# A residual block of two quantised 3x3 convolutions on one core: second weights transposed between the phases, the last phase's loads reordered, one totals addition moved

## The chip, the cores and the metric

The kernel runs on one core of one Trainium2 chip. The metric is the device time of one execution in microseconds (us).

## What is computed

The input x has 32 images of 128 channels and 56 by 56 pixels, all float32. Two convolutions of 3x3 taps (padding 1) follow one another; their weights are rounded to eight integer levels (-4 to 3) times a step alpha. Behind each stands a batch normalisation over all images, so that no image of the second convolution can start before the last of the first is done.

```
residual = x
out = conv3x3_decomposed(x, lsq_quantize(w1, alpha1))
out = jax.nn.relu(batchnorm(out, gamma1, beta1))
out = conv3x3_decomposed(out, lsq_quantize(w2, alpha2))
out = batchnorm(out, gamma2, beta2)
out = jax.nn.relu(out + residual)
```

## The kernel before, in words

The channels lie on the 128 partitions. An image is one row of 3136 float32 per partition. Ten slots in SBUF hold images; the other 22 results of each convolution are spilled to DRAM and come back.

**Phases.** Phase 1 is the first convolution for images 0 to 31, phase 2 the second (steps 32 to 63). The last phase applies the second normalisation, adds x, applies ReLU and stores. Between phases 1 and 2, `batchnorm_affine` (L767) makes scale and bias from the totals.

**One image.** Rows 0 to 35 are computed by a Winograd scheme with six products, rows 36 to 55 directly in three chunks of nine taps. Every operand is split into a high and a low part (`v_hi`, `v_lo`, `d_hi`, `d_lo`), so each tap is two matmuls. TensorE runs `chunk` (L914, 54 matmuls) into PSUM banks 6 and 7 and `products` (L886, 36 matmuls) into banks 0 to 5. VectorE (`step`, L750) makes `q_rows`, `p_rows` and `v_rows` of the next image, the low parts `d_lo` (L691) and of the first pair `v_lo` (L686), and from the products the output rows: `first_difference` (L697), `second_difference` (L705), `second_sum` (L711), `rows_out` (L716). `add_totals` (L737) adds an image's sums to the totals; it needs ScalarE's three squares of that image (L512). ScalarE (`step`, L521) copies chunks and products out of PSUM, squares, and casts the high parts. GpSimd subtracts the low parts of the second and third pair (L422), two instructions per image.

**Weights.** VectorE rounds the weights to integers in bfloat16 and sums taps for the Winograd scheme (`sum_taps`, L257; for w2 in images 3 to 8). TensorE transposes them in lots (`transpose_lot`, L879) into PSUM, and ScalarE copies them to `w1T` or `w2T` with a scale (`take`, L438). w2 has three lots of 8, 8 and 5 transposes, all into bank 7. In before they stand in images 10, 11 and 12 of phase 1, behind the last chunk (`lot_of_w2`, L946), and the next image's first chunk, which needs bank 7, waits for the copies (L964). ScalarE takes them behind the high parts of the next image (L538).

**Order of the work.** Each engine's program is written by hand, with semaphores counted up. Explicit images come first (`EXPLICIT` = 14 for all three engines), then a loop of two images a turn. SyncE issues the transfers strictly in its own order: an instruction that waits holds up all behind it. In the last phase the x of 32 images is loaded into seven buffers, `xbuf`. They lie over memory of the convolutions, and each load waits for its last use (L368 to L391):

```
AT = [0, PIX, 2 * PIX, 3 * PIX, 4 * PIX, 5 * PIX]
TEMPS = 5 * PIX + 2 * ((D_PLANE + 7) // 8 * 8)
xbuf = [placed(f"xbuf{b}", PIX, F32, b * PIX)[:, :] for b in range(ARENA_XBUFS)]
xbuf.append(nc.alloc_sbuf_tensor_at("xbuf_w2", [C, PIX], F32, offset=w2_base)[:, :])
```

`AT` holds the places of `w1T`, `q_rows` and `p_rows`, `v_rows`, `v_hi`, `v_lo`, and the two `d` planes; `m1`, `m3`, `d1`, `s1` begin at `TEMPS`. So buffer 5 lies over `d_hi`, `d_lo`, `m1` and part of `m3`, and buffer 6 over `w2T`. `FINAL` (L268) is the order of the last phase; image j of it uses buffer j % 7. `load_y2` (L363) reloads a spilled result into the slot of image j - 6 as soon as that one's output is stored.

Of the kernel before, what the change touches and what calls it, by code (L numbers as in the profile page):

```python
# [27 lines left out]
def residual_block(nc, x, w1, alpha1, gamma1, beta1, w2, alpha2, gamma2, beta2, out):  # L28
# [48 lines left out]
    with ExitStack() as ctx:  # L77
# [32 lines left out]
        xbuf.append(nc.alloc_sbuf_tensor_at("xbuf_w2", [C, PIX], F32, offset=w2_base)[:, :])  # L110
# [125 lines left out]
        W_BANK = [[0, 1, 2, 3], [7, 7, 7]]  # L236
        W2_FIRST = 10
        EXPLICIT = 14
# [45 lines left out]
        def _(sp):  # L284
# [91 lines left out]
            load_residual(2)  # L376

            sp.wait_ge(chunk_done, STEPS * NC)
            sp.wait_ge(sums_ready, STEPS * SR)
            load_residual(5)  # L380

# [3 lines left out]
            for b in range(2):  # L385
                sp.wait_ge(y2_stored[b], 16 * (SPILL // 2))


            sp.wait_ge(m_done, STEPS * M)
            sp.wait_ge(chunk_done, STEPS * NC)  # L390
# [43 lines left out]
        def _(act):  # L434
# [86 lines left out]
            def step(g, p, b, phase, first=False, second=False, last=False, input_ready=None, relu_next=None,  # L521
                     w2_lot=None):
                if not last:
                    input_ready()
                    hi_direct(g + 1, p + 1)
                take_chunk(g, p, b, NC - 1)
                take_m(g, 0)
                if second:
                    act.wait_ge(shift_ready, phase + 1)
                if not first:  # L530
                    square(g - 1, p + (SLOTS - 1), 1 - b, phase, 0)
                take_m(g, 1)
                if not first:
                    square(g - 1, p + (SLOTS - 1), 1 - b, phase, 1)
                    square(g - 1, p + (SLOTS - 1), 1 - b, phase, 2)
                if not last:
                    hi_pairs(g + 1)
                if w2_lot is not None:  # L538
                    take_w2(w2_lot)
                if relu_next is not None:  # L540
                    relu_next()
                if not last:

                    if not first:
                        act.wait_ge(totalled, g)
                    for j in range(NC - 1):
                        take_chunk(g + 1, p + 1, 1 - b, j)
# [18 lines left out]
            for n in range(2, EXPLICIT):  # L566
                phase1(n, n % 2, n // 2, w2_lot=n - W2_FIRST if n in range(W2_FIRST, W2_FIRST + 3) else None)
            with act.Fori(EXPLICIT // 2, (IMAGES - 2) // 2) as i:
                for b in range(2):
                    phase1(i * 2 + b, b, i)  # L570
            phase1(IMAGES - 2, 0, (IMAGES - 2) // 2)
            step(IMAGES - 1, IMAGES - 1, 1, 0, last=True)
            finish_phase(IMAGES - 1, IMAGES - 1, 1, 0)

# [52 lines left out]
        def _(dve):  # L627
# [122 lines left out]
            def step(g, p, b, phase, first=False, input_ready=None):  # L750
# [7 lines left out]
                if not first:  # L758
# [4 lines left out]
                rows_out(g, p, b)  # L763
                if first:
# [113 lines left out]
        def _(pe):  # L878
# [67 lines left out]
            def lot_of_w2(n):  # L946
                def transposes(j):
                    if j == NC - 1:
                        pe.wait_ge(w_int_ready[1], 2)
                        pe.wait_ge(evac_done, n * NC + 2)  # L950
                        transpose_lot(1, n - W2_FIRST)
                return transposes
# [8 lines left out]
            for n in range(1, EXPLICIT):  # L961
                if n in range(W2_FIRST + 1, W2_FIRST + 4):

                    pe.wait_ge(wT_ready, TAKES + (2, 5, TAKES)[n - 1 - W2_FIRST])  # L964
                convolve(n, wT[0], lot_of_w2(n) if n in range(W2_FIRST, W2_FIRST + 3) else None)
            with pe.Fori(EXPLICIT // 2, IMAGES // 2) as i:
                for b in range(2):
                    convolve(i * 2 + b, wT[0])
            convolve(IMAGES, wT[1])
# [25 lines left out]
```

## Time and profile before

| what | value |
|---|---|
| median of 3 runs | 1489.55 us (1488.96 to 1489.67) |
| the profiled execution's own time | 1491.95 us |
| its span, first to last instruction | 1490.0 us |
| TensorE busy | 1136.8 us, 76% |
| VectorE busy | 1141.8 us, 77% |
| ScalarE busy | 855.4 us, 57% |
| GpSimd busy | 306.3 us, 21% |
| HBM read and written | 174.59 MB and 122.03 MB |

The profile is one execution. Its busy time is the time in which an engine had an instruction in work, and its times count from the first instruction. "Idle before" an instruction is put down to what it waited for last. The engines are named PE (TensorE), PEld (its weight loads), DVE (VectorE), ACT (ScalarE), POOL (GpSimd) and SP (SyncE); a q behind the name is the engine's queue that issues transfers.

### The profile page before, as it was taken

How to read it: one execution, taken by the hardware profiler on the slowest of the kernel's cores; microseconds unless marked ns; L12 is line 12 of the kernel's file. 1: busy time of each engine (PE TensorE's matmuls, PEld its weight loads, DVE VectorE, ACT ScalarE, POOL GpSimd, SP SyncE). 2: the span in 40 equal slices, each digit the busy share in tenths (PEclk: the TensorE clock that was granted, in tenths of full speed). 3: DMA queues.
4: the chain of work that ended last, by engine and by line, in shares of the span. 5: the costliest groups of instructions: out<-in, count | busy, mean ns of one | idle time of the engine just before them, and what ended most of it. 6: DMA issues, size and time to landing. Idle time of an engine off the chain costs nothing.

```text
span 1490.0 us, 18697 instructions
## 1 busy us (share of the span) xinstructions
PE 1136.8 (76%) x5802; PEld 1033.1 (69%) x5802; DVE 1141.8 (77%) x1626; ACT 855.4 (57%) x1263; POOL 306.3 (21%) x147
## 2 busy tenths in 40 slices
PE   5999998999999999699999999999999400000000
PEld 5999987999999998699999999999999400000000
DVE  7999996788888886898888888888888632322324
ACT  3555555555556565677777777777777532222224
POOL 3333221122222222322222222222222100000000
PEclk9999999999999999899999999999999855555555
DMA  3455443455542220022244455554230699999999
GB/s 162 168 189 196 184 173 118 152 196 187 198 186 86 86 86 0 1 87 87 86 172 172 172 194 194 192 196 170 89 129 5 246 428 430 430 430 430 429 429 408
DMA packets 28110, 297.00 MB, mean 199 GB/s; under 512 B 3888, under 2 KB 3888, under 8 KB 4912
## 3 DMA queue, kind: packets, MB, share of 16 engines
q1 hardware_dynamic: 22608, 245.25, 41.7%
q10 hardware_dynamic: 5472, 51.38, 8.1%
q8 instruction: 15, 0.25, 0.1%
q14 instruction: 15, 0.12, 0.0%
HBM read 174.59 MB, written 122.03 MB: 199 GB/s over the span
## 4 chain that ended last, share of the span: by engine, by line
issue 64%; DMA 18%; POOL 14%; DVE 1%; ACT 1%; POOLq 1%; ACTq 0%; DVEq 0%
POOL v_lo L422 14%; DMA slots<-conv_spill 10%; DMA out<-slots 4%; DMA xbuf<-in_x 3%; DVE slots L872 1%; ACT slots L619 1%; POOLq L427 0%; POOLq L421 0%; POOLq L77 0%; POOLq L422 0%; ACTq L623 0%; DVE affine L793 0%; DVE tiny L790 0%; DVE affine L792 0%; POOL ident L408 0%
## 5 line engine op out<-in xcount | busy, mean ns | idle before, releaser
L422 POOL TENSOR_TENSOR v_lo<-v_rows,v_hi 128x1008 fp32r<-128x1008 f32 x128 | 304.0, 2395 | 835.1 <-ACT v_hi L474 835.1
L925 PE MATMUL conv_psum<-d_hi,w1T 128*128 128x398 f32 (+2 forms) x864 | 289.0, 338 | 11.0 <-ACT w2T L440 8.1
L925 PE MATMUL conv_psum<-d_hi,w2T 128*128 128x398 f32 (+2 forms) x864 | 285.8, 335 | 12.4 <-DVE d_lo L691 12.4
L925 PE MATMUL conv_psum<-d_lo,w1T 128*128 128x398 f32 (+2 forms) x864 | 286.6, 336 | 0.0
L925 PE MATMUL conv_psum<-d_lo,w2T 128*128 128x398 f32 (+2 forms) x864 | 284.1, 333 | 0.0
L512 ACT ACTIVATE squares<-slots,minus_shift 128x1008 bf16 (+3 forms) x192 | 225.0, 1172 | 13.7 <-ACT squares L512 8.9
L905 PE MATMUL conv_psum<-v_lo,w1T 128*128 128x512 f32 x576 | 227.1, 394 | 0.0
L905 PE MATMUL conv_psum<-v_lo,w2T 128*128 128x512 f32 x576 | 227.0, 394 | 0.0
L905 PE MATMUL conv_psum<-v_hi,w2T 128*128 128x512 f32 x576 | 226.8, 394 | 0.3 <-POOL v_lo L422 0.2
L905 PE MATMUL conv_psum<-v_hi,w1T 128*128 128x512 f32 x576 | 226.8, 394 | 0.0
L619 ACT ACTIVATE slots<-slots,affine 128x3136 f32<-128x3136 f32 (+1 forms) x34 | 93.6, 2754 | 209.1 <-DVE slots L872 208.3
L872 DVE SCALAR_TENSOR_TENSOR slots<-slots,affine,xbuf 128x3136 f32<-128x3136 f32 (+1 forms) x30 | 97.4, 3265 | 151.4 <-DMA slots<-conv_spill 146.7
L493 ACT ACTIVATE slots<-conv_psum 128x392 f32 (+3 forms) x192 | 91.4, 476 | 187.8 <-PE conv_psum L925 186.6
L474 ACT CAST v_hi<-v_rows 128x1008 fp32r<-128x1008 f32 x192 | 186.1, 1028 | 6.7 <-DVE v_rows L673 5.8
L691 DVE TENSOR_TENSOR d_lo<-slots,d_hi 128x1176 fp32r<-128x1176 f32 x64 | 90.7, 1416 | 110.3 <-ACT d_hi L479 110.3
L925 PEld LDWEIGHTS conv_psum<-d_hi,w1T 128*128 128x128 f32 x864 | 165.2, 191 | 14.0 <-ACT w2T L440 9.4
L925 PEld LDWEIGHTS conv_psum<-d_hi,w2T 128*128 128x128 f32 x864 | 163.2, 189 | 14.1 <-DVE d_lo L691 12.8
L925 PEld LDWEIGHTS conv_psum<-d_lo,w1T 128*128 128x128 f32 x864 | 165.6, 192 | 1.2
L925 PEld LDWEIGHTS conv_psum<-d_lo,w2T 128*128 128x128 f32 x864 | 163.6, 189 | 1.2
L479 ACT CAST d_hi<-slots 128x1176 fp32r (+1 forms) x64 | 75.6, 1180 | 139.0 <-PE conv_psum L925 133.5
L649 DVE SCALAR_TENSOR_TENSOR q_rows<-slots 128x2016 f32 (+1 forms) x64 | 144.3, 2255 | 0.8 <-ACT slots L518 0.5
L905 PEld LDWEIGHTS conv_psum<-v_lo,w1T 128*128 128x128 f32 x576 | 108.7, 189 | 24.1
(79 smaller groups left out, 1511.3 us busy)
## 6 DMA issues: line engine op xcount, KB each, us to landing
conv_spill<-slots SPq DMA_DIRECT2D x44, 1568.0 KB, 6.1
slots<-conv_spill SPq DMA_DIRECT2D x44, 1568.0 KB, 10.8
slots<-in_x SPq DMA_DIRECT2D x31, 1568.0 KB, 8.9
out<-slots ACTq DMA_DIRECT2D x30, 1568.0 KB, 11.7
xbuf<-in_x SPq DMA_DIRECT2D x28, 1568.0 KB, 52.0
xbuf_w<-in_x SPq DMA_DIRECT2D x4, 1568.0 KB, 51.6
out<-slots ACTq DMA_DIRECT2D x4, 784.0 KB, 10.5
slots<-in_L_conv_w SPq DMA_DIRECT2D x2, 576.0 KB, 9.7
```

Source lines behind the costliest of these rows:

```text
L422: nc.gpsimd.tensor_tensor(pair_window(1, k), pair_rows(k), pair_window(0, k).bitcast(F32), ALU.subtract).then_inc(pool_lo_ready, 1)
L474: nc.scalar.copy(pair_window(0, k), pair_rows(k)).then_inc(hi_ready, 1)
L479: nc.scalar.copy(window(d_plane[0], 0, D_ROWS), rows_of(slot(p + SLOTS, WINO - 1))).then_inc(hi_ready, 1)
L493: nc.scalar.activation(rows_of(slot(p + SLOTS, r0, r1)), bank_rows(CHUNK_BANK[j], r1 - r0), ACT.Identity, accum_out=sums[b][:, col:col + 1 ...
L512: nc.scalar.activation(into, y, ACT.Square, bias=minus_shift[:, phase:phase + 1], accum_out=sums[b][:, col:col + 1]).then_inc(squared, 1)
L619: nc.scalar.activation(z, z, ACT.Relu, bias=affine[:, 1, 1:2]).then_inc(final_ready, 1)
L649: return nc.vector.scalar_tensor_tensor(out=out, in0=in0, scalar=scalar, in1=in1, op0=ALU.mult, op1=ALU.add)
L691: nc.vector.tensor_tensor(window(d_plane[1], 0, D_ROWS), rows_of(slot(p, WINO - 1)), window(d_plane[0], 0, D_ROWS).bitcast(F32), ALU.subtr ...
L872: nc.vector.scalar_tensor_tensor(out=z, in0=z, scalar=affine[:, 1, 0:1], in1=xbuf[b][:, r0 * W:r1 * W], op0=ALU.mult, op1=ALU.add).then_in ...
L905: last = nc.tensor.matmul(bank_run(M_BANK[k], TILES), w[:, M_WEIGHT[k] + kw, :], run(v_plane[half], k * TILES, (k + 1) * TILES, kw - 1), s ...
L925: last = nc.tensor.matmul(bank_run(CHUNK_BANK[j], r1 - r0), w[:, kh * 3 + kw, :], run(d_plane[half], r0 - WINO + 1, r1 - WINO + 1, kw - 1) ...
```

## The change

The three lots of w2 leave phase 1. TensorE transposes them behind the last image of phase 1, into banks 6, 7 and 0, and ScalarE copies them behind its last squares. Images 2 to 31 of TensorE and ScalarE are now turns of the loop, on VectorE images 10 to 31. The buffer over `w2T` becomes number 5, and the one over `d_hi`, `d_lo`, `m1` and `m3` number 6; the last loads are issued in the order 3, 4, 5, 6. In the last step of each phase the totals of the image before are added behind the output rows.

```diff
-        xbuf.append(nc.alloc_sbuf_tensor_at("xbuf_w2", [C, PIX], F32, offset=w2_base)[:, :])
+        xbuf.insert(5, nc.alloc_sbuf_tensor_at("xbuf_w2", [C, PIX], F32, offset=w2_base)[:, :])
...
-        W_BANK = [[0, 1, 2, 3], [7, 7, 7]]
-        W2_FIRST = 10
-        EXPLICIT = 14
+        W_BANK = [[0, 1, 2, 3], [6, 7, 0]]
+        EXPLICIT = 10
...
             load_residual(2)
+            for b in range(2):
+                sp.wait_ge(y2_stored[b], 16 * (SPILL // 2))
 
             sp.wait_ge(chunk_done, STEPS * NC)
-            sp.wait_ge(sums_ready, STEPS * SR)
-            load_residual(5)
-
             sp.wait_ge(m_done, STEPS * M)
             load_residual(3)
             load_residual(4)
-            for b in range(2):
-                sp.wait_ge(y2_stored[b], 16 * (SPILL // 2))
-
-
-            sp.wait_ge(m_done, STEPS * M)
-            sp.wait_ge(chunk_done, STEPS * NC)
+            load_residual(5)
+
+            sp.wait_ge(sums_ready, STEPS * SR)
             load_residual(6)
...
-                if w2_lot is not None:
-                    take_w2(w2_lot)
...
-            for n in range(2, EXPLICIT):
-                phase1(n, n % 2, n // 2, w2_lot=n - W2_FIRST if n in range(W2_FIRST, W2_FIRST + 3) else None)
-            with act.Fori(EXPLICIT // 2, (IMAGES - 2) // 2) as i:
+            with act.Fori(1, (IMAGES - 2) // 2) as i:
...
             finish_phase(IMAGES - 1, IMAGES - 1, 1, 0)
+            for h in range(3):
+                take_w2(h)
...
-                if not first:
+                if not first and input_ready is not None:
                     add_totals(g - 1, 1 - b, phase)
                 if input_ready is not None:
                     lo_of_pair(g + 1, 0)
                 second_sum(g)
                 rows_out(g, p, b)
+                if input_ready is None:
+                    add_totals(g - 1, 1 - b, phase)
...
+            def second_weights():
+
+                pe.wait_ge(w_int_ready[1], 2)
+                pe.wait_ge(evac_done, IMAGES * NC)
+                pe.wait_ge(m_copied, IMAGES * 2 - 1)
+                for h in range(3):
+                    transpose_lot(1, h)
+                pe.wait_ge(wT_ready, 2 * TAKES)
...
             convolve(0, wT[0], rest_of_w1)
-            for n in range(1, EXPLICIT):
-                if n in range(W2_FIRST + 1, W2_FIRST + 4):
-
-                    pe.wait_ge(wT_ready, TAKES + (2, 5, TAKES)[n - 1 - W2_FIRST])
-                convolve(n, wT[0], lot_of_w2(n) if n in range(W2_FIRST, W2_FIRST + 3) else None)
-            with pe.Fori(EXPLICIT // 2, IMAGES // 2) as i:
+            convolve(1, wT[0])
+            with pe.Fori(1, IMAGES // 2) as i:
                 for b in range(2):
                     convolve(i * 2 + b, wT[0])
+            second_weights()
             convolve(IMAGES, wT[1])
```

TensorE, in image 10 of phase 1 in the program before (`ident,w_int` is a transpose of w2's integers):

```order
L925 MATMUL conv_psum<-d_hi,w1T 128x284
L925 MATMUL conv_psum<-d_lo,w1T 128x284
L882 MATMUL conv_psum<-ident,w_int 128x128 [waits evac_done,w2_int_ready]
L882 MATMUL conv_psum<-ident,w_int 128x128 x7
L905 MATMUL conv_psum<-v_hi,w1T 128x512 [waits m_copied,lo_ready]
L905 MATMUL conv_psum<-v_lo,w1T 128x512
```

The eight transposes stand between the last chunk and the products; images 11 and 12 have the same piece. In the changed program these images have no such rows.

TensorE, the end of phase 1's loop and the start of phase 2 in the changed program:

```order
L899 MATMUL conv_psum<-v_lo,w1T 128x512
L957 REGISTER_ALU
L957 COMPARE_AND_BRANCH
L876 MATMUL conv_psum<-ident,w_int 128x128 [waits m_copied,evac_done,w2_int_ready]
L876 MATMUL conv_psum<-ident,w_int 128x128 x20
L919 MATMUL conv_psum<-d_hi,w2T 128x398 [waits evac_done,lo_ready,wT_ready]
L919 MATMUL conv_psum<-d_lo,w2T 128x398
```

The lots stood between chunks and products of three images; now all 21 transposes stand behind the loop, and only the first chunk of phase 2 waits for wT_ready.

ScalarE, the end of phase 1 and the start of phase 2 in the changed program (`squares,sums` are the last squares, `slots<-slots,affine` is the ReLU of phase 2):

```order
L507 ACTIVATE squares,sums<-slots,minus_shift 128x1120 [waits evac_done,squared]
L507 ACTIVATE squares,sums<-slots,minus_shift 128x1008 [waits rows_ready,squared] x2
L435 ACTIVATE w2T<-conv_psum 128x1024 [waits transposed]
L435 ACTIVATE w2T<-conv_psum 128x384
L435 ACTIVATE w2T<-conv_psum 128x128 [waits transposed]
L435 ACTIVATE w2T<-conv_psum 128x768
L435 ACTIVATE w2T<-conv_psum 128x128
L435 ACTIVATE w2T<-conv_psum 128x640 [waits transposed]
L513 ACTIVATE slots<-slots,affine 128x1176 [waits affine_ready]
L474 CAST d_hi<-slots 128x21x56 [waits chunk_done,relu_ready]
L513 ACTIVATE slots<-slots,affine 128x1960
```

In the program before, the ReLU with its wait for affine_ready stood right behind the last squares; the six copies are new here.

SyncE, the loads of the first seven images' x for the last phase (`xbuf_62` is buffer 0, `xbuf_w_68` the one over w2T, `xbuf_67` the one over d_hi, d_lo, m1 and m3), in the program before:

```order
L361 DMA xbuf_62<-in_x 128x3136 [waits m_done]
L361 DMA xbuf_63<-in_x 128x3136 [waits v_ready]
L361 DMA xbuf_64<-in_x 128x3136 [waits pool_lo_ready,lo_ready]
L361 DMA xbuf_67<-in_x 128x3136 [waits sums_ready,chunk_done]
L361 DMA xbuf_65<-in_x 128x3136 [waits m_done]
L361 DMA xbuf_66<-in_x 128x3136
L361 DMA xbuf_w_68<-in_x 128x3136 [waits m_done,chunk_done,y2_stored1,y2_stored0]
L361 DMA xbuf_62<-in_x 128x3136 [waits added]
```

The load of buffer 5 with its wait for sums_ready stands ahead of those of buffers 3 and 4.

And in the changed program:

```order
L360 DMA xbuf_62<-in_x 128x3136 [waits m_done]
L360 DMA xbuf_63<-in_x 128x3136 [waits v_ready]
L360 DMA xbuf_64<-in_x 128x3136 [waits pool_lo_ready,lo_ready]
L360 DMA xbuf_65<-in_x 128x3136 [waits chunk_done,m_done,y2_stored1,y2_stored0]
L360 DMA xbuf_66<-in_x 128x3136
L360 DMA xbuf_w_68<-in_x 128x3136
L360 DMA xbuf_67<-in_x 128x3136 [waits sums_ready]
L360 DMA xbuf_62<-in_x 128x3136 [waits added]
```

The wait for sums_ready stood ahead of four loads and now stands ahead of one.

## Rows read from the trace of the kernel before

**Rows 1.** The page, the span in 40 slices: busy share of the DMA engines.

```profile
DMA  3455443455542220022244455554230699999999
```

**Rows 2.** Busy time by stage: PE, PEld, DVE, ACT, POOL, clock, DMA share, GB/s.

```profile
215.00:220.00 5.00, 4.19 (x15) 4.18 (x16) 4.90 (x11) 0.76 (x2) 3.40 (x2) 0.66 0.96 326
335.00:580.00 245.00, 245.00 (x1257) 223.08 (x1256) 216.10 (x335) 143.03 (x252) 60.83 (x29) 1.00 0.34 127
1170.00:1175.00 5.00, 2.97 (x13) 2.08 (x11) 3.80 (x9) 4.20 (x8) 0.00 (x0) 1.00 0.00 2
1180.00:1490.00 310.00, 0.00 (x0) 0.00 (x0) 112.19 (x38) 93.63 (x34) 0.10 (x1) 0.50 1.00 426
```

**Rows 3.** Who waited for whom, TensorE only: total, times, longest us.

```profile
PE conv_psum L925 <- ACT w2T L440: 8.1, 3, 3.0
```

**Rows 4.** Timeline of TensorE, images 9 to 31: start us, length us.

```profile
186.19 0.39 PE L905 MATMUL conv_psum<-v_hi,w1T 128*128 128x512 f32 x1
...
194.53 0.35 PE L925 MATMUL conv_psum<-d_hi,w1T 128*128 128x398 f32 x1
...
203.76 0.62 PE L882 MATMUL conv_psum<-ident,w_int 128*128 128x128 bf16 x8
...
215.81 0.70 PE L925 MATMUL conv_psum<-d_hi,w1T 128*128 128x398 f32 x1 [3.02 <-ACT w2T L440]
...
288.68 0.39 PE L905 MATMUL conv_psum<-v_hi,w1T 128*128 128x512 f32 x1
...
587.31 0.39 PE L905 MATMUL conv_psum<-v_hi,w1T 128*128 128x512 f32 x1
```

**Rows 5.** Timeline of TensorE, the start of phase 2.

```profile
608.24 0.70 PE L925 MATMUL conv_psum<-d_hi,w2T 128*128 128x398 f32 x1 [12.42 <-DVE d_lo L691]
```

**Rows 6.** Timeline of ScalarE, the copies of the three lots of w2.

```profile
214.37 1.39 ACT L440 ACTIVATE w2T<-conv_psum 128x1024 fp32r<-128x1024 bf16 x2
...
237.22 1.13 ACT L440 ACTIVATE w2T<-conv_psum 128x128 fp32r<-128x128 bf16 x3
...
259.70 0.69 ACT L440 ACTIVATE w2T<-conv_psum 128x640 fp32r<-128x640 bf16 x1
```

**Rows 7.** Timeline of VectorE and ScalarE, from phase 1 to phase 2.

```profile
593.15 0.69 DVE L709 TENSOR_TENSOR conv_psum<-m,conv_psum 128x504 f32<-128x504 f32 x1 [1.48 <-PE conv_psum L905]
594.73 0.17 DVE L740 TENSOR_TENSOR totals<-totals,sums 128x10 f32<-128x10 f32 x1 [0.90 <-ACT squares L512]
594.82 0.68 DVE L714 TENSOR_TENSOR conv_psum<-m,conv_psum 128x504 f32<-128x504 f32 x1
...
604.20 1.37 ACT L518 ACTIVATE slots<-slots,affine 128x1176 f32<-128x1176 f32 x1 [3.60 <-DVE affine L793]
```

**Rows 8.** Timeline of TensorE and VectorE, the end of phase 2.

```profile
1172.58 0.39 PE L905 MATMUL conv_psum<-v_lo,w2T 128*128 128x512 f32 x1
...
1174.36 0.67 DVE L649 SCALAR_TENSOR_TENSOR s<-conv_psum,s 128x504 f32<-128x504 f32 x1
```

**Rows 9.** Timeline of SyncE's queue, the first loads of the last phase.

```profile
1175.11 0.80 SPq L361 DMA_DIRECT2D xbuf<-in_x  x2
...
1184.87 0.33 SPq L361 DMA_DIRECT2D xbuf<-in_x  x1
```

**Rows 10.** Timeline of GpSimd and VectorE, images 9 to 16.

```profile
189.34 1.38 DVE L691 TENSOR_TENSOR d_lo<-slots,d_hi 128x1176 fp32r<-128x1176 f32 x1
195.52 5.36 POOL L422 TENSOR_TENSOR v_lo<-v_rows,v_hi 128x1008 fp32r<-128x1008 f32 x2 [12.21 <-ACT v_hi L474]
195.90 1.84 DVE L740 TENSOR_TENSOR totals<-totals,sums 128x10 f32<-128x10 f32 x1
...
213.00 0.16 DVE L740 TENSOR_TENSOR totals<-totals,sums 128x10 f32<-128x10 f32 x1
213.61 4.79 POOL L422 TENSOR_TENSOR v_lo<-v_rows,v_hi 128x1008 fp32r<-128x1008 f32 x2 [12.73 <-ACT v_hi L474]
...
315.68 4.41 POOL L422 TENSOR_TENSOR v_lo<-v_rows,v_hi 128x1008 fp32r<-128x1008 f32 x2 [13.15 <-ACT v_hi L474]
```

More of the change, by code:

```diff
@@ L519, in relu, with step @@
                                      scale=affine[:, 0, 0:1]).then_inc(relu_ready, 1)
-            def step(g, p, b, phase, first=False, second=False, last=False, input_ready=None, relu_next=None,
-                     w2_lot=None):
+            def step(g, p, b, phase, first=False, second=False, last=False, input_ready=None, relu_next=None):
                 if not last:
@@ L944, in rest_of_w1 @@
                     pe.wait_ge(wT_ready, TAKES)
[L946 to L952, printed above, removed]
+            def second_weights():
[5 more added lines that the diff above has]
+                pe.wait_ge(wT_ready, 2 * TAKES)
             pe.wait_ge(ident_ready, 1)
```

## The prediction

> **What bounds the kernel now.** I read the bands of the page first, then the busy time by stage, then who waits for whom, and last the timelines at the three places that the change touches. The DMA band [rows 1] shows a kernel of two kinds: 31 slices with the DMA engines partly idle, then a last phase in which they are full. The table by stage [rows 2] says the same: between 335 and 580 us TensorE is busy for 245.00 of 245 us, and from 1180 us on it is not used and the DMA share is 1.00. So the convolutions last as long as TensorE's instructions plus its waits, and the last phase as long as its bytes plus its late start. Whatever gives TensorE a wait back, or starts the last phase's transfers sooner, should show in the end; most other edits should not.
>
> TensorE's waits on the way are few: 8.1 us in three pieces for the copies of w2T [rows 3], and 12.42 us between the phases for the first d_lo [rows 5].
>
> **Term 1, the lots of w2 leave images 10 to 12.** The first matmul of products marks each image [rows 4]. From image 14 to image 31 it moves 587.31 - 288.68 = 298.63 us over 17 images, 17.567 us each. From image 9 to image 14 it moves 102.49 us where five such images take 87.83. The excess, 14.66 us, is what the three lots cost, more than the 8.1 us of waits. The rest has two parts. One is the transposes themselves: the eight of a lot take 0.62 us at 203.76, so all 21 take under 1.9 us. The other is the clock: the first wait ends at 215.81, and from 215 to 220 us the mean granted clock is 0.66 [rows 2], that is, a part of them at 1.2 GHz instead of 2.4. These matmuls follow one another at twice their distance until the clock is back. All of it goes with the lots, since nothing else in images 10 to 12 has been added and TensorE, as the bound, passes it on in full. **-14.66 us.**
>
> The unrolled images become turns of a loop on TensorE and ScalarE (from image 2) and on VectorE (from image 10). In before, images 14 to 31 are such turns, and TensorE is busy for every one of 245 us of them, so the loop itself costs nothing that can be seen; I cost it at nothing, with a small rival below.
>
> **Where the lots go.** The 21 transposes stand behind the last products, under 1.9 us of an idle stretch of 12.42 us [rows 5]. The six copies take 1.39 + 1.13 + 0.69 = 3.21 us [rows 6]. They stand on ScalarE between the last square of phase 1 and the first ReLU, where it waited 3.60 us for the affine numbers [rows 7]. Term 2 brings the last square and the affine numbers forward by the same amount, so the cover stays 3.60 us and 0.39 us of it is left. The transposes are done before the last squares are, so the copies need not wait. Cost 0; without the cover it is the 3.21 us of the copies, in front of the ReLU, the first d_hi, the first d_lo and so TensorE. A gain here is excluded: ScalarE waits there either way. TensorE's new wait for all copies ends some 4 us before that d_lo.
>
> **Term 2, the totals of the last image but one.** In the last step VectorE reaches this addition with its first difference done at 593.15 + 0.69 = 593.84 us and waits for a square until 594.73; the second sum follows at 594.82 [rows 7]. Without the addition in front, the second sum needs only the difference before it. The nearest dependent pair is in [rows 8]: an operation ends at 1174.36 + 0.67 = 1175.03, and SyncE, which waits for its semaphore, issues at 1175.11 [rows 9], 0.08 us later; I take 0.1. The second sum then starts at 593.95, 0.87 us sooner, and the four output rows, the last square, the last totals, the affine numbers and the first ReLU of phase 2 with it. The moved addition (0.17 us) comes behind the last rows, while ScalarE squares; hidden. **-0.87 us** at the first boundary. The same happens at the second boundary, but behind it the DMA engines set the end, not the affine numbers, so I count nothing there.
>
> **Term 3, loads of the last phase.** In before, load 5 stood ahead of 3 and 4 and waited for the very last use of s1; SyncE takes its instructions in order, so all four loads are issued from 1175.11 on [rows 9]. From 1170 to 1175 us the DMA share is 0.00 [rows 2]. Now 3, 4 and 5 need only the last matmul, which ends at 1172.58 + 0.39 = 1172.97 us [rows 8]; with 0.1 us for the semaphore they are issued from 1173.07, and only load 6 waits for s1. Three loads are 4.8 MB, at the 426 GB/s of [rows 2] some 11 us of work, so load 6 and the load issued at 1184.87 [rows 9] find the engines still busy, as before. Each image's output is then issued faster than it is stored. The queue never runs dry, the bytes are the same, and the end moves by the start: 1175.11 - 1173.07 = **-2.04 us**. At worst this is 0, if something other than bytes sets the pace of the last phase. At best the 0.87 us of term 2 are worth something too. The waits for stores of y2, moved ahead, are for transfers issued long before: nothing.
>
> **Sum.** -14.66 - 0.87 - 2.04 = -17.57 us. The profiled execution took 1491.95 us with a span of 1490.0 us, so it would take 1474.4 us. The median of the runs shown, 1489.55 us, is 2.4 us below the profiled one; I take the same difference off it: **1472.0 us**.
>
> **Rivals.**
> 1. The copies lie open. The slack is 0.39 us, worked out from three copies' groups in another place. For it: ScalarE also has to see the semaphores of three lots. Against it: all of these are up when it arrives. Time 1472.0 + 3.2 = 1475.2 us. Chance 7%.
> 2. The reordered loads bring nothing, because the last phase is tied by its chain of add, ReLU, output and reload of a slot. For it: VectorE waits for reloads there all the time. Against it: the DMA share is 1.00 all along. Time 1474.0 us. Chance 7%. With rival 1 together 1477.2 us.
> 3. The change doesn't do what it says for phase 1: the three lots gave VectorE time to catch up, and without them TensorE waits elsewhere. For it: in images 3 to 9 VectorE runs late. Its totals addition takes 1.84 us at 195.90, while GpSimd's subtraction has run since 195.52, against 0.16 us at 213.00 [rows 10]. Against it: that image was reached before the first stall, which ends at 215.81, so VectorE had caught up by itself; from 195.90 to 213.00 it took 17.10 us, 0.47 us less than TensorE's 17.57. But without the transposes GpSimd would start at 195.52 + 17.57 = 213.09 instead of 213.61, only 0.09 us behind that addition. Being late costs nothing at first: d_lo was done at 190.72 us, and TensorE takes it up at 194.53, a cushion of 3.8 us. If VectorE stays late in a milder way, 1 or 2 us are lost: 1473.5 us, chance 4%.
> 4. **The slow end.** The same lateness feeds itself: two VectorE subtractions of each image come to stand behind a whole GpSimd subtraction of 4.41 / 2 = 2.2 us. Its round is then 17.10 - 1.68 + 4.4 = 19.8 us, 2.25 us over TensorE's, in 22 images (10 to 31) 49.6 us, less the cushion 45.8 us: 1472.0 + 45.8 = 1518 us. It turns the gain into a loss from (17.57 + 3.8) / 22 = 0.97 us an image on. Against it: images 3 to 9 were late with one such block and a round below 17.57 us, and later GpSimd's pair takes 4.41 us, unhindered. Chance 2%.
>
> The Trainium skill ("SBUF — State Buffer", section "Who interferes with whom") states the rule behind rivals 3 and 4: a VectorE instruction with two SBUF inputs and a GpSimd instruction that reads SBUF share a port under an exclusive lock, and the later one waits for the whole of the earlier. By that rule the 0.09 us decide who waits, and the time would go towards rival 4 if VectorE lost each time. The row with 1.84 us agrees with the lock; the full rounds of TensorE through images 3 to 9 speak against a cost.
>
> **How the numbers follow.** My forecast has 78%, rivals 1 to 4 have 7, 7, 4 and 2%, and 2% is left for things not thought of. The forecast's own spread is about 1 us each way, for the offset to the median, the length of the slow clock behind the first wait of phase 2, and the tail; term 2 counted twice gives 1471.1. With rivals 1 and 2, together too, the range is **1469.5 to 1477.2 us**. About 0.2% (3 us) is what a measurement of this kernel can tell from no change. All cases but the fourth and part of the unknown are faster by more: faster 0.96, same 0.01, slower 0.03.
>
> **What would show it.** Right: images 9 to 14 at 17.57 us each, no wait of TensorE for w2T, the granted clock whole in phase 1; the six copies between 599.7 and 603.3 us of the old times, which is 14.66 us earlier in the new profile, followed by a small wait of ScalarE for the affine numbers; the second sum right behind the difference; three residual loads some 0.1 us after the last matmul, and no idle slice of DMA behind them. Wrong: totals additions of 1.8 us and longer past image 9, a ReLU that starts when the last copy ends, or a DMA share under 1.00 in the last phase.

## The result, and the profile after

| what | before | after |
|---|---|---|
| median | 1489.61 us (1488.96 to 1489.82) | 1474.51 us (1474.09 to 1474.73) |
| the profiled execution's own time | 1491.95 us | 1474.38 us |
| its span | 1490.0 us | 1472.6 us |

The ratio is 0.9899 (95% interval 0.9882 to 0.9916): 15.1 us faster. The forecast was 1472.0 us, with 1469.5 to 1477.2 as its range. The profiled executions are 17.57 us apart, which is the forecast's sum to the hundredth; the medians are not. Both facts are looked into below: the agreement to the hundredth is partly luck, and the difference between profile and median belongs to the first term.

The page after, of the two bands that answer to [rows 1]:

```profile
PEclk9999999999999999899999999999999755555555
DMA  4354454444452210022245555444230799999999
```

The last phase still begins in the 32nd slice, and its first slice is fuller (7 for 6). By stage, to be held against [rows 2] (columns as there):

```profile
200.00:560.00 360.00, 360.00 (x1848) 327.97 (x1847) 327.56 (x498) 208.74 (x368) 92.33 (x41) 1.00 0.39 147
1163.00:1168.00 5.00, 0.00 (x0) 0.00 (x0) 4.29 (x10) 0.00 (x0) 0.55 (x1) 0.52 1.01 432
1180.00:1470.00 290.00, 0.00 (x0) 0.00 (x0) 96.69 (x30) 84.07 (x31) 0.00 (x0) 0.50 1.01 429
```

TensorE is busy for 360.00 of 360 us, with a granted clock of 1.00, where [rows 2] had 0.66 from 215 to 220 us. Its waits after, as [rows 3]:

```profile
PE conv_psum L876 <- DVE slots L250: 12.5, 1, 12.5
PE conv_psum L919 <- issue: 10.3, 1, 10.3
PE conv_psum L919 <- ACT slots L488: 1.4, 1, 1.4
PE conv_psum L919 <- ACT w1T L435: 1.2, 1, 1.2
PE conv_psum L899 <- POOL v_lo L417: 0.2, 1, 0.2
```

The waits for w2T, 8.1 us, are gone, and no wait in images 1 to 31 has come in their place. The first, third and fourth rows are the start of the kernel, the last is image 33. The second is the boundary between the phases: 21 transposes and 10.34 us idle where [rows 5] had 12.42. The timeline of TensorE there:

```profile
581.65 1.35 PE L876 MATMUL conv_psum<-ident,w_int 128*128 128x128 bf16 x21
593.33 0.67 PE L919 MATMUL conv_psum<-d_hi,w2T 128*128 128x398 f32 x1 [10.34 <-issue]
```

ScalarE, which answers to [rows 6] and the last of [rows 7]:

```profile
585.55 3.01 ACT L435 ACTIVATE w2T<-conv_psum 128x1024 fp32r<-128x1024 bf16 x6
589.24 1.37 ACT L513 ACTIVATE slots<-slots,affine 128x1176 f32<-128x1176 f32 x1 [0.68 <-DVE affine L787]
```

The six copies take 3.01 us where 3.21 was forecast, and ScalarE still waits 0.68 us for the affine numbers. VectorE, the first difference and second sum of [rows 7], and the moved addition:

```profile
579.13 0.69 DVE L701 TENSOR_TENSOR conv_psum<-m,conv_psum 128x504 f32<-128x504 f32 x1 [1.48 <-PE conv_psum L899]
579.85 0.69 DVE L706 TENSOR_TENSOR conv_psum<-m,conv_psum 128x504 f32<-128x504 f32 x1
...
584.24 0.17 DVE L732 TENSOR_TENSOR totals<-totals,sums 128x10 f32<-128x10 f32 x1
```

The sum starts 0.03 us behind the end of the difference (0.1 was forecast). SyncE's queue at the start of the last phase, as [rows 9]; the last matmul of phase 2 ends at 1158.02:

```profile
1158.12 0.80 SPq L360 DMA_DIRECT2D xbuf<-in_x  x2
1158.97 0.43 SPq L360 DMA_DIRECT2D xbuf_w<-in_x  x1
1159.44 9.85 SPq L360 DMA_DIRECT2D xbuf<-in_x  x2
```

Three loads go out from 0.10 us behind that end, as forecast. GpSimd in images 13 to 15 and VectorE's totals additions in images 11 and 13, for [rows 10]:

```profile
266.54 5.37 POOL L417 TENSOR_TENSOR v_lo<-v_rows,v_hi 128x1008 fp32r<-128x1008 f32 x2 [11.89 <-ACT v_hi L469]
284.12 5.28 POOL L417 TENSOR_TENSOR v_lo<-v_rows,v_hi 128x1008 fp32r<-128x1008 f32 x2 [12.21 <-ACT v_hi L469]
301.67 4.41 POOL L417 TENSOR_TENSOR v_lo<-v_rows,v_hi 128x1008 fp32r<-128x1008 f32 x2 [12.28 <-ACT v_hi L469]
```

```profile
231.75 1.89 DVE L732 TENSOR_TENSOR totals<-totals,sums 128x10 f32<-128x10 f32 x1
...
266.80 1.97 DVE L732 TENSOR_TENSOR totals<-totals,sums 128x10 f32<-128x10 f32 x1
```

In this execution VectorE stayed late without the lots, as rivals 3 and 4 feared: pairs of 5.3 us go on to image 14, and totals additions of over 1.8 us stand in images 11 and 13. The prediction had named such additions past image 9 as a sign that it was wrong. TensorE's full 360 us say that they cost nothing. They are no mark of the change either: the changed kernel profiled once more, in the same span within 0.1 us, is not late at all.

```profile
266.62 4.42 POOL L417 TENSOR_TENSOR v_lo<-v_rows,v_hi 128x1008 fp32r<-128x1008 f32 x2 [13.14 <-ACT v_hi L469]
```

### The profile page after: what moved, and what is told of

Same layout as the page of the kernel before. It is cut to its first block, busy times and chain, and to the rows that moved or that the text cites. A ratio compares the mean times of both kernels' runs of the same rounds, so it can differ in the third digit from the quotient of the medians.

```text
span 1472.6 us, 19012 instructions
## 1 busy us (share of the span) xinstructions
PE 1132.3 (77%) x5802; PEld 1030.2 (70%) x5802; DVE 1150.9 (78%) x1626; ACT 855.3 (58%) x1263; POOL 306.7 (21%) x147
## 4 chain that ended last, share of the span: by engine, by line
issue 62%; DMA 18%; POOL 14%; DVE 2%; ACT 2%; PE 1%; POOLq 1%; SPq 0%; ACTq 0%; DVEq 0%
POOL v_lo L417 14%; DMA slots<-conv_spill 11%; DMA out<-slots 4%; DMA xbuf<-in_x 3%; DVE slots L866 1%; ACT slots L611 1%; PE conv_psum L919 1%; DMA slots<-in_L_conv_w 0%; POOLq L422 0%; ACT v_hi L469 0%; ACT w1T L435 0%; DVE slots L250 0%; POOLq L416 0%; PE conv_psum L876 0%; ACT d_hi L474 0%
## 5 line engine op out<-in xcount | busy, mean ns | idle before, releaser
L919 PE MATMUL conv_psum<-d_hi,w2T 128*128 128x398 f32 (+2 forms) x864 | 285.9, 335 | 10.3 <-issue 10.3
```

What stands on the lines that cost most here:

```text
L919: last = nc.tensor.matmul(bank_run(CHUNK_BANK[j], r1 - r0), w[:, kh * 3 + kw, :], run(d_plane[half], r0 - WINO + 1, r1 - WINO + 1, kw - 1) ...
```

## The experiments

All times are medians. Ratios are to runs of the kernel before made beside them on the same chip; those had medians of 1490.22 us beside the first four kernels below, 1490.08 beside the next four, 1489.88 beside the three with or next to the warm boundary and 1489.96 beside the last. Single executions of the kernel before scatter from 1489.0 to 1494.5 us. "Marks" are the starts of an image's first products matmul in the timeline, as in the prediction. A "slow" matmul is one of TensorE's chunks (128x398 and smaller) that takes over 0.5 us where most take 0.35; the granted clock is then at the lower of its two levels, 1.2 GHz.

### The same program again

Unchanged code.

> The kernel before once more, unchanged, for a second profiled execution beside the first. The measured change was -15.1 us in the runs' medians, while the two profiled spans lie 1490.0 - 1472.6 = 17.4 us apart, close to the -17.57 us that was forecast. Theory A (the profiled execution of before was an unlucky one: its TensorE spent longer at 1.2 GHz behind the stalls of the three w2 lots than usual): a new profiled span near 1487.7 us, and images 9 to 14 take some 12.3 us more than five steady ones, not 14.66. Theory B (the three lots always cost 14.66 us, and the changed kernel lost some 2.4 us elsewhere): a span near 1490 us again in profiled executions, or images 9 to 14 at 14.7 us of excess again at a shorter span.

**Measured:** 1489.78 us (1489.09 to 1493.94), ratio 0.9999 (0.999 to 1.0008), span 1487.8 us, 2.2 us under the first profile of the same program. The excess of images 9 to 13 over 87.83 us is 11.86 us, not 14.66. That is 2.80 us less where the span is 2.2 us less; image 0 took 0.52 us more this time (its products begin at 28.61 us and not at 28.09). The windows around the second lot's stall show why. First the kernel before in its first profile, then in this one (columns: PE, clock, DMA share, GB/s):

```profile
236.00:244.00 8.00, 5.60 (x22) 0.79 1.00 376
```

```profile
236.00:244.00 8.00, 5.24 (x29) 1.00 0.98 370
```

The wait is 2.76 us in both timelines. Behind it the granted clock fell in one execution and not in the other.

### One part of the change alone

Lots and loops only:

```diff
-        xbuf.insert(5, nc.alloc_sbuf_tensor_at("xbuf_w2", ...
+        xbuf.append(nc.alloc_sbuf_tensor_at("xbuf_w2", ...
...
-                if not first and input_ready is not None:
+                if not first:
                     add_totals(g - 1, 1 - b, phase)
...
-                if input_ready is None:
-                    add_totals(g - 1, 1 - b, phase)
```

(against the changed kernel, with the loads too in their old order).

> Only the three lots of w2 moved behind phase 1 (with the loops as in the change); loads and totals as before. Theory A: -12.3 us or so against before in the medians (ratio 0.9917). Theory B: -14.7 us (0.9901). Rival of the exposed copies: the last totals come 0.87 us later than in the change, but so do the affine numbers, so the copies stay under the wait of 3.6 us; if they lay open, 3 us less gain.

Totals only, against before:

```diff
-                if not first:
+                if not first and input_ready is not None:
                     add_totals(g - 1, 1 - b, phase)
...
                 rows_out(g, p, b)
+                if input_ready is None:
+                    add_totals(g - 1, 1 - b, phase)
```

> Only the totals addition of the last step of each phase moved behind the output rows. My theory: -0.87 us, once, at the first boundary, and nothing at the second, where the DMA engines set the end (ratio 0.9994). Rival: it counts at both boundaries, -1.7 us (0.9988).

Loads only, against before:

```diff
-        xbuf.append(nc.alloc_sbuf_tensor_at("xbuf_w2", ...
+        xbuf.insert(5, nc.alloc_sbuf_tensor_at("xbuf_w2", ...
...
+            for b in range(2):
+                sp.wait_ge(y2_stored[b], 16 * (SPILL // 2))
             sp.wait_ge(chunk_done, STEPS * NC)
-            sp.wait_ge(sums_ready, STEPS * SR)
-            load_residual(5)
             sp.wait_ge(m_done, STEPS * M)
             load_residual(3)
             load_residual(4)
-            for b in range(2):
-                sp.wait_ge(y2_stored[b], 16 * (SPILL // 2))
-            sp.wait_ge(m_done, STEPS * M)
-            sp.wait_ge(chunk_done, STEPS * NC)
+            load_residual(5)
+            sp.wait_ge(sums_ready, STEPS * SR)
             load_residual(6)
```

> Only the buffers 5 and 6 exchanged and the last phase's first loads reordered. My theory: three loads issued 2.04 us earlier and all of it seen at the end, -2.0 us (ratio 0.9986). Rival (the last phase is tied by its chain of add, ReLU, output and reload): 0.

**Measured.** "Tail" is the span's end (given to 0.1 us) less TensorE's last end; "boundary" is the mark of image 33 less that of image 31.

| kernel | median, us | ratio | excess of images 9 to 13 | slow matmuls behind the three stalls | boundary | tail |
|---|---|---|---|---|---|---|
| before, first profile | 1489.61 | | 14.66 | 9, 10, 8 | 50.16 | 317.03 |
| before again | 1489.78 | 0.9999 | 11.86 | 9, 0, 0 | 50.16 | 317.09 |
| totals only | 1487.85 | 0.9983 (0.9974 to 0.9991) | 16.03 | 10, 17, 9 | 49.28 | 316.23 |
| loads only | 1487.64 | 0.9979 (0.997 to 0.9989) | 13.21 | 0, 10, 8 | 50.16 | 314.56 |
| lots only | 1478.30 | 0.9913 (0.9901 to 0.9926) | 0.00 | no stall | 50.15 | 317.03 |
| the change | 1474.51 | 0.9899 (0.9882 to 0.9916) | 0.00 | no stall | 49.21 | 314.58 |

Each part moves what it touches. Beside that, the clock behind the stalls varies, and the start of image 0: its products begin between 28.09 and 29.20 us in these six profiles, and by nothing that was edited. The lots are worth 1489.78 - 1478.30 = 11.5 us, or 11.9 us against all runs of the kernel before made beside them: the excess of the second profile and not of the first. This rests on medians of a kernel that scatters; the interval of the ratio alone, 11.0 to 14.8 us, would still touch 14.66. The totals give 0.88 us at the boundary, and alone 0.86 us (0.80 against the first profile) in the tail as well, because there the old loads wait for s1, which comes sooner (they go out 1.19 us behind the last matmul, not 2.14); with the new loads that part is not counted again. The loads give 2.47 us of tail. In medians the totals alone and the loads alone brought 2.4 and 2.6 us against 1490.22 us, each with an interval of about 1.3 us either way, so it is the marks and tails that tell these small parts, not the medians.

### Are the loops free?

Images 2 to 13 written out again on TensorE and ScalarE, and 10 to 13 on VectorE, in the changed kernel:

```diff
-        EXPLICIT = 10
+        EXPLICIT = 14
...
-            convolve(1, wT[0])
-            with pe.Fori(1, IMAGES // 2) as i:
+            for n in range(1, EXPLICIT):
+                convolve(n, wT[0])
+            with pe.Fori(EXPLICIT // 2, IMAGES // 2) as i:
```

> The changed kernel with images 2 to 13 written out again on TensorE and ScalarE and 10 to 13 on VectorE, as in the kernel before, w2 still behind phase 1. If the loops cost nothing, as I took it: 1474.5 us, ratio to before as the change has it (0.99), images 9 to 14 at 17.57 us each. If turns of the loop were slower than written-out images or kept VectorE late: up to 1 us less.

**Measured:** 1474.50 us (1473.92 to 1475.16) against 1474.51; images 9 to 13 at 17.57 us in both. The loops cost nothing.

### The copies made twice

```diff
             for h in range(3):
                 take_w2(h)
+            act.wait_ge(wT_ready, 2 * TAKES)
+            for k, h, first, end, plane, scale in ((1, 0, 0, 8, 0, SCALE), ...
+                take(k, h, first, end, plane, scale)
...
-                pe.wait_ge(wT_ready, 2 * TAKES)
+                pe.wait_ge(wT_ready, 3 * TAKES)
```

> The changed kernel with the six copies of w2T between the phases made twice. In the profile of the change they take 3.01 us and ScalarE waits another 0.68 us for the affine numbers behind them. If that wait is the cover, the second round of 3.0 us (and about 0.1 us for its semaphore) shows less 0.68 us: +2.4 us against the change, 1476.9 us. If ScalarE were not on the path at all: 0. If the copies already lay open: the full +3.1 us.

**Measured:** 1476.16 us (1475.9 to 1477.38), boundary 51.48 us, 2.27 us longer than with one set. ScalarE's timeline:

```profile
585.41 6.09 ACT L435 ACTIVATE w2T<-conv_psum 128x1024 fp32r<-128x1024 bf16 x12
591.33 1.41 ACT L513 ACTIVATE slots<-slots,affine 128x1176 f32<-128x1176 f32 x1
```

3.08 us more of copies, less the slack of 0.68, is 2.40 us, and the boundary shows 2.27 of it. So the first set lies wholly in cover (rival 1 falls), and a second lies open but for that slack. The median rose by 1.65 us only: in this profile image 0 was 0.15 us shorter and the tail 0.3 us shorter than in the change, for which no run gives a reason.

### The stalls filled

In before, 44 transposes of the identity into bank 6 behind the wait for its evacuation, ahead of each wait for w2T:

```diff
+                    pe.wait_ge(evac_done, n * NC)
+                    for t in range(FILL):
+                        nc.tensor.transpose(psum[:, 6, :] ... ident[:, :], ident[:, :])
                     pe.wait_ge(wT_ready, TAKES + (2, 5, TAKES)[n - 1 - W2_FIRST])
```

> The kernel before, with 44 transposes of the identity (0.055 us each, into the free bank 6) put into each of TensorE's three waits for the copies of w2T. They change nothing but TensorE's activity. In four profiled executions so far, images 9 to 14 took 14.66, 11.86, 16.03 and 13.20 us more than steady ones, with slow matmuls behind 3, 1, 3 and 2 of the three waits; rounds without slow matmuls add up to 0.43 + 3.80 + 3.38 + 2.68 = 10.3 us. If the clock makes the difference: no slow matmul in images 11 to 13, an excess near 10.3 us in the profile, a median 1 to 2 us under the kernel before (ratio 0.999), and no runs 4 us above it. If something else does: the same scatter from 1489 to 1494.5 us.

**Measured:** 1488.27 us (1487.65 to 1489.46), ratio 0.9984 (0.9975 to 0.9993). The excess is 10.29 us, with no slow matmul behind any stall. The same window as above, in this kernel:

```profile
236.00:244.00 8.00, 7.71 (x58) 1.00 0.90 328
```

TensorE was kept at work and its clock stayed whole. So 10.3 us of the excess are stalls and transposes, and what lies above (1.6 to 5.7 us in the table) is clock. The scatter says the same: the eleven executions of this kernel lie within 1.8 us, the 29 of the kernel before within 5.3 us, and the four of the change, which has no such stall, within 0.7 us.

### Loads by the part of a buffer that comes free

Buffer 6 in two pieces (over the `d` planes once the chunks are done, the rest behind s1), and the first halves of buffers 3 and 4 once three of the last six products are done:

```diff
             sp.wait_ge(chunk_done, STEPS * NC)
+            load_part(6, 0, planes)
+            sp.wait_ge(m_done, STEPS * M - 3)
+            load_part(3, 0, half)
+            load_part(4, 0, half)
             sp.wait_ge(m_done, STEPS * M)
-            load_residual(3)
-            load_residual(4)
+            load_part(3, half, PIX)
+            load_part(4, half, PIX)
             load_residual(5)
             sp.wait_ge(sums_ready, STEPS * SR)
-            load_residual(6)
+            load_part(6, planes, PIX)
...
```

> The changed kernel with three of the last phase's first loads split where their memory comes free in parts: the columns of buffer 6 over d_hi and d_lo behind the last chunk, the first halves of buffers 3 and 4 (over v_hi and v_lo) behind the third of the last six products, the rest as before. 1.23 MB and 1.57 MB move into the stretch in which the DMA engines stood still. At 426 GB/s that is 6.6 us: 1467.9 us. If the last phase were tied by its chain and not by bytes: 0.

**Measured:** 1470.15 us (1469.9 to 1471.0), ratio 0.9864 (0.9849 to 0.988): 4.4 us under the change, not 6.6. Stretches of 5 us, first of the change and then of this kernel (columns: clock, DMA share, GB/s):

```profile
1153.00:1158.00 5.00, 1.00 0.00 2
1158.00:1163.00 5.00, 1.00 0.78 268
1163.00:1168.00 5.00, 0.52 1.01 432
1168.00:1173.00 5.00, 0.50 1.00 429
```

```profile
1153.00:1158.00 5.00, 1.00 0.94 342
1158.00:1163.00 5.00, 0.82 0.91 350
1163.00:1168.00 5.00, 0.50 1.02 427
1168.00:1173.00 5.00, 0.50 0.87 296
```

The idle 5 us are filled. From 1168 to 1173 us (429 - 296) x 5 = 0.67 MB, 1.6 us of work, are missing: the loads have run out before the first outputs follow. That holds most of the missing 2.2 us. Not all of the 4.4 us is the split: in the profiles the tail is 3.6 us shorter, and 0.55 us come from a shorter image 0, which the edit doesn't touch.

### A warm clock at the boundary

The first chunk of phase 2 begins at 1.2 GHz (9 slow matmuls in the change; the granted clock from 587 to 592 us is 0.50). Here 165 transposes of the identity into bank 1 fill the idle stretch, in the changed kernel:

```diff
+                pe.wait_ge(sums_ready, (IMAGES - 1) * SR + 2)
+                for t in range(165):
+                    nc.tensor.transpose(psum[:, 1, :] ... ident[:, :], ident[:, :])
                 pe.wait_ge(wT_ready, 2 * TAKES)
```

> The changed kernel with 165 transposes of the identity (0.055 us each, 9 us) into the free bank 1 behind those of w2, so that TensorE is not idle before phase 2. In the profiles so far the first chunk of phase 2 runs 8 to 16 matmuls at the slow distance, some 0.15 us lost at each. If these were on the path, 1.2 to 1.8 us would be gained. But from the products of image 31 to those of image 33 all profiles with the same cover show the same time whatever the number of slow matmuls (49.21 us with 9 and with 8, 49.28 with 12; 50.16 in before with 9 and with 11), so my theory is that VectorE and GpSimd set that stretch: 0, 1474.5 us, and still 49.2 us between the two marks.

The changed kernel once more, beside it:

> The changed kernel once more, beside the two above, for their comparison: 1474.5 us, runs within 1 us of each other, since only the starts of image 0 and of phase 2 have slow matmuls left.

The warm boundary again, with the split loads and 110 such transposes at the kernel's start:

> The split loads (1470.15 us so far), the boundary kept busy, and 110 transposes of the identity ahead of the first lot of w1, while TensorE waits for the weights at the start. In all profiles the first chunk of image 0 has 8 to 17 slow matmuls, and the first products of image 0 come at 28.1 to 29.2 us in step with them, 0.11 us a matmul. Without them, if nothing else sets image 0: some 27.2 us, so 1 to 2 us under the split loads alone, 1468.2 to 1469.2 us, and less scatter from run to run. If VectorE's planes for the products set image 0: 0.

**Measured:** 1478.49 us (1477.8 to 1478.78) for the first, 4.0 us slower than the change; 1473.74 (1473.62 to 1473.86) for the second, 3.6 us slower than the split loads alone. The changed kernel run again beside the first gave 1474.47 us (1474.16 to 1474.64). With the transposes the granted clock from 587 to 592 us was 1.00, no matmul at the boundary was slow any more, and image 32's products came 1.4 us sooner; but the boundary took 52.75 us, 3.5 us more than in the change. The rest of the 4.0 us is in the tail (0.6 us), unexplained. The transposes at the start did nothing: image 0 had 12 slow matmuls, where the other profiles have 8 to 17, behind two waits of 2.7 and 1.2 us that stayed (granted clock 0.59 from 15 to 20 us). The rows name the new wait. TensorE's waits, GpSimd and VectorE with the warm boundary:

```profile
PE conv_psum L899 <- POOL v_lo L417: 3.9, 1, 3.9
```

```profile
600.99 8.65 POOL L417 TENSOR_TENSOR v_lo<-v_rows,v_hi 128x1008 fp32r<-128x1008 f32 x1 [12.91 <-ACT v_hi L469]
```

```profile
600.65 1.20 DVE L678 TENSOR_TENSOR v_lo<-v_rows,v_hi 128x1008 fp32r<-128x1008 f32 x1
601.77 2.25 DVE L641 SCALAR_TENSOR_TENSOR q_rows<-slots 128x2016 f32<-128x2016 f32 x1
603.94 1.20 DVE L658 TENSOR_TENSOR p_rows<-slots 128x1008 f32<-128x1008 f32 x1
605.06 1.38 DVE L683 TENSOR_TENSOR d_lo<-slots,d_hi 128x1176 fp32r<-128x1176 f32 x1
606.35 0.68 DVE L664 TENSOR_TENSOR v_rows<-q_rows 128x504 f32<-128x504 f32 x1
606.95 0.68 DVE L665 TENSOR_TENSOR v_rows<-q_rows 128x504 f32<-128x504 f32 x1
```

And GpSimd and VectorE in the changed kernel:

```profile
600.89 6.21 POOL L417 TENSOR_TENSOR v_lo<-v_rows,v_hi 128x1008 fp32r<-128x1008 f32 x1 [12.90 <-ACT v_hi L469]
```

```profile
603.84 1.20 DVE L658 TENSOR_TENSOR p_rows<-slots 128x1008 f32<-128x1008 f32 x1
605.59 2.76 DVE L683 TENSOR_TENSOR d_lo<-slots,d_hi 128x1176 fp32r<-128x1176 f32 x1 [0.54 <-ACT d_hi L474]
```

In the change VectorE waits 0.54 us for the high part of `d`, and GpSimd's subtraction goes through in that gap (it ends at 607.10, and VectorE's d_lo, which begins meanwhile, takes twice its 1.38 us). With the warm clock the high part is there in time, VectorE leaves no gap until 607.63, and GpSimd ends at 609.64, 2.54 us later, with TensorE waiting. That GpSimd gets through in the gap is read from these times; the next experiment tests that VectorE is what holds it off.

### The gap given back

In the kernel of all three, VectorE waits for both of GpSimd's subtractions of image 32 before it starts on image 33:

```diff
             first_planes(IMAGES, SPILL)
+            dve.wait_ge(pool_lo_ready, (IMAGES + 1) * PLO)
             phase2(0, 0, first=True)
```

> The kernel all_three with one wait more: VectorE doesn't begin on image 33 (q_rows) before GpSimd has subtracted both its pairs of image 32. Theory (the port): in all_three TensorE's wait of 4.0 us for GpSimd's v_lo comes from VectorE, whose two-input instructions then follow one another without a gap from 600.65 us on (in the kernel with the boundary warmed alone) until d_lo of image 33 and two rows of v_rows are written, at 607.63; GpSimd's first subtraction, begun at 600.99, ends only at 609.64, 2.0 us behind the last of them. With the wait GpSimd should do its two subtractions of about 2.1 us each right away, TensorE's wait for v_lo should be 0 to 0.3 us, and the products of image 33 should follow those of image 31 by 47.0 to 48.5 us instead of 52.77. Time 1473.74 - 4.3 to 5.8 = 1467.9 to 1469.4 us. Rival A (GpSimd is late for a reason of its own, not VectorE): its first subtraction still takes over 6 us and the time stays at 1473.7 us or above. Rival B (VectorE, which starts image 33 some 4 us later, becomes the bound): no wait for v_lo, but the gain is eaten by waits of TensorE for VectorE's d_lo or sums, 1472 to 1474 us.

**Measured:** 1469.09 us (1468.69 to 1469.5), ratio 0.9855 (0.9838 to 0.9872): 4.65 us less by one wait more. TensorE no longer waits for v_lo, and the boundary takes 48.36 us. GpSimd and VectorE:

```profile
600.33 5.02 POOL L427 TENSOR_TENSOR v_lo<-v_rows,v_hi 128x1008 fp32r<-128x1008 f32 x2 [12.90 <-ACT v_hi L479]
```

```profile
605.38 2.26 DVE L651 SCALAR_TENSOR_TENSOR q_rows<-slots 128x2016 f32<-128x2016 f32 x1 [4.18 <-POOL v_lo L427]
```

Both subtractions now take 5.02 us together. The cause is settled: GpSimd was held off by VectorE. TensorE's waits for ScalarE are 1.3 us longer than in the kernel of all three (2.7 for 1.4), so some of what the warm clock gives is still lost. This is the best kernel of the study, 5.4 us under the change. Of that, 4.4 us came with the split loads; the warm clock, the transposes at the start and the gap together are worth 1.1 us over these (1470.15 us), and the boundary says the same (48.36 for 49.25). The gap without the warm clock was not tried. It might bring as much, since in the change too GpSimd's subtraction takes 6.21 us there.

## Why the prediction was right, and where its size was off

**What bounds the kernel** held: TensorE's waits and the last phase's start account for the difference. Between the two profiles, -14.66 in images 9 to 13, -0.94 at the boundary and -2.47 in the tail (from unrounded spans) make -18.07 us, and image 0, 0.65 us longer in the profile after, leaves -17.42, which is the difference of the spans (the executions' own times add 0.15). So the agreement to the hundredth is partly luck: terms 2 and 3 were 0.5 us short together, and the start of the kernel took that back.

**The number** came out 2.5 us over the forecast, outside the "about 1 us each way" of the forecast's own spread. It lies in the range because the range's upper part was held open for rivals 1 and 2 (1475.2 and 1474.0 us), and neither of them came true. That the range held is luck as well.

**Term 1, -14.66 us,** had the right mechanism and the wrong size; this is the term that was mis-sized. "All of it goes with the lots" is true, but "the excess, 14.66 us," is one execution's. Of the three stalls' slow matmuls, 27 in the profile read, a second profile of the same code had 9, with an excess of 11.86. The lots alone brought 11.5 us. The text had the warning in its hands: the profiled execution lay 2.4 us above the median. "I take the same difference off it" moved that offset to the changed kernel as if it were part of any profile. It was part of the very term that was removed: 2.8 us of slow clock behind the second and third stall. The profiled execution after lies 0.1 us under its median. Taken off the term instead, 14.66 - 2.40 = 12.26, the forecast would have been 1489.55 - 12.26 - 0.87 - 2.04 = 1474.4 us. With the second profile's 11.86 it is 1474.8 us.

**The lots' new place, 0 us,** held. The cover was 3.69 us where 3.60 was taken, with 0.68 us left, since the copies took 3.01 us. Rival 1 is refuted, by the profile and by the second set of copies.

**The loops, 0 us,** held: written out, they give the same time.

**Term 2, -0.87 us,** held: -0.95 in the change and -0.88 alone, at the boundary. "I count nothing" at the second boundary was right for the change, and wrong where the old loads stay, as the run alone showed.

**Term 3, -2.04 us,** was 0.4 us short: 317.03 - 314.58 = 2.45 us. The issue came 0.10 us behind the last matmul, as forecast. Where the other 0.4 us come from was not isolated. Rival 2 is refuted: the last phase is tied by its bytes and their start, and split loads shorten it further.

**Rivals 3 and 4** tied VectorE's lateness to the lots, and that was wrong. In the profile after it stayed late to image 13, with a cushion of 2.1 us left at d_lo of image 11 (done at 210.63 us, taken up at 212.75), and cost nothing. But the same code was not late in its second profile, nor was the kernel with the lots alone moved; and with the lots still in phase 1, the kernels with totals only and with loads only were not late either. In all 14 profiles it goes with the first subtraction of GpSimd for image 0: in five it takes 2.24 to 2.28 us and no totals addition takes over 0.5 us, in nine it takes 5.63 to 6.44 us and VectorE is late up to image 9, 11 or 13. What decides between the two is open. No profile of either kind has a wait of TensorE for it in phase 1.

The Trainium skill ("SBUF — State Buffer", section "Who interferes with whom") has the later of the two sharers of the port wait for the whole of the earlier. The trace agrees at the boundary that one waits for the other, but shows a wait for more than one instruction: GpSimd's subtraction began at 600.99 us, VectorE's instruction then in work ended at 601.85, and GpSimd came through at 609.64 only, 2.0 us behind the end of five more of VectorE's, back to back. That is 8.65 us for a subtraction that needs some 2.2, and two took 5.02 us once VectorE stood aside. That this can cost time was seen only where TensorE had no cushion.

## What to carry to other kernels

Before reading a term from a profile, hold the profiled execution's own time against the median: what it lies above belongs to whatever was unlucky in it, and if that is what a change removes, the offset comes off the term and not off the end. A second profile of the same code tells what varies by itself; here that was the clock behind the stalls, the start of image 0 and VectorE's lateness. A stall of TensorE costs its idle time each time and its clock in some executions. An engine brought forward can take away a gap in which another one got through; if a speed-up turns into a wait elsewhere, look at who shares a port, and give the gap back at a point of your choice.

## What the hardware showed unexpectedly

- **The clock behind a stall is not repeatable.** Behind equal waits of 3.02, 2.76 and 2.32 us, four profiles show 0 to 17 slow matmuls, and an excess of 11.86 to 16.03 us; the code of these images is the same in all four. What decides it stays open.
- **Slow matmuls can be free.** The distance from image 31 to 33 is 50.15 to 50.16 us with 8, 9 and 11 of them at phase 2's start, and 49.21 to 49.28 us, with the totals moved, with 8, 9, 12 and 15. That VectorE and GpSimd set the pace there fits this. One profile, of the filled stalls, had 16 and 50.39 us; the 0.24 us are not explained. Removed alone, they made the kernel 4.0 us slower.
- **Losing a gap of 0.54 us on VectorE went with a boundary 3.5 us longer**, as GpSimd's subtraction had gone through in it; standing VectorE aside on purpose brought 4.65 us.
- **Transposes hold the clock.** TensorE kept busy with transposes of the identity has a granted clock of 1.00 from 587 to 592 us, where the idle engine has 0.50.
